# Straight code instead of loops on five engines, and a per-partition scalar in GpSimd's row normalisation, in an attention block with a LoRA mixture behind it

## The reference, cut to what matters

```python
x = x + attn(_layernorm(x), Wq, Wk, Wv, Wo, q_norm_w, k_norm_w)     # x: (2, 1024, 512)
x = x + lora_mixture(_layernorm(x), A, B, Wr, br)
...
q = rmsnorm(x @ Wq.T)      # 32 heads of 128
k = rmsnorm(x @ Wk.T)      # 8 heads of 128, each shared by 4 query heads
v = x @ Wv.T
scores = einsum(q, k) / sqrt(128) + alibi_bias          # causal
attn = softmax(scores)
out = einsum(attn, v) @ Wo.T
```

## Time and profile before

| | |
|---|---|
| timed runs | 2343.06, 2344.05, 2346.43 us; median 2344.05 us |
| span of the profiled execution | 2337.8 us |
| PE matmuls, busy | 2204.3 us, 94% of the span |
| PE weight loads, busy | 1901.5 us, 81% |
| DVE busy | 1403.3 us, 60% |
| ACT busy | 1185.4 us, 51% |
| POOL busy | 912.3 us, 39% |
| mean granted TensorE clock | 0.975 |
| DMA | 53.40 MB, 23 GB/s over the span |

### The profile page before, as it was taken

The page is one execution under the profiler, slowest core; times in us unless marked ns, Lnnn a source line. Parts: engine busy times, 40 slices in busy tenths (PEclk is TensorE's granted clock), DMA queues, the critical chain, the costliest instruction groups (busy, mean ns, idle before and its releaser), DMA issues.

```text
span 2337.8 us, 39513 instructions
## 1 busy us (share of the span) xinstructions
PE 2204.3 (94%) x12540; PEld 1901.5 (81%) x12540; DVE 1403.3 (60%) x3492; ACT 1185.4 (51%) x3397; POOL 912.3 (39%) x912
## 2 busy tenths in 40 slices
PE   6999999999999999999869999999999999999997
PEld 5887888878788887888668878787887888878885
DVE  4655656656565655656656556565565656656666
ACT  3554545555454555645235556454554545555552
POOL 3344343434343343444124434334343343434341
PEclk9999999999999999999989999999999999999999
DMA  3001010010101001010120010100001010010000
GB/s 118 19 1 46 1 46 1 13 34 1 46 1 43 4 1 46 1 46 1 47 67 7 1 46 1 47 1 28 19 1 46 1 46 1 1 46 1 1 1 37
DMA packets 27914, 53.40 MB, mean 23 GB/s; under 512 B 3033, under 2 KB 3033, under 8 KB 27745
## 3 DMA queue, kind: packets, MB, share of 16 engines
q1 hardware_dynamic: 26112, 50.34, 6.5%
q10 hardware_dynamic: 1632, 0.55, 0.1%
HBM read 46.68 MB, written 4.19 MB: 22 GB/s over the span
## 4 chain that ended last, share of the span: by engine, by line
PE 83%; issue 9%; POOL 4%; DVE 1%; ACT 1%; DMA 0%; ACTq 0%; POOLq 0%; DVEq 0%
PE s_ps L863 23%; PE turn_ps L855 17%; PE o_ps L863 16%; PE q_ps L863 14%; PE y_ps L863 13%; POOL probs L612 3%; DVE pT_lo L688 1%; ACT qn L531 1%; POOL q_inv_t L583 1%; DMA bias<-in_L_ffn_B 0%; ACT pT_hi L488 0%; POOL rstd L583 0%; POOL q_sum_eps_t L581 0%; PE q_ps L1013 0%; POOL bias L622 0%
## 5 line engine op out<-in xcount | busy, mean ns | idle before, releaser
L612 POOL TENSOR_TENSOR probs<-probs,p_inv_t 128x896 f32<-128x896 f32 (+7 forms) x512 | 576.7, 1147 | 724.7 <-DVE p_inv_t L756 724.7
L488 ACT ACTIVATE pT_hi<-turn_ps 128x512 fp32r<-128x512 f32 x576 | 332.7, 600 | 487.2 <-PE turn_ps L855 486.2
L748 DVE CUSTOM_DVE_ANT_0 probs<-s_ps,bias 128x896 f32<-128x896 f32 (+7 forms) x512 | 382.2, 753 | 187.2 <-issue 184.6
L688 DVE TENSOR_TENSOR pT_lo<-turn_ps,pT_hi 128x512 fp32r<-128x512 f32 x576 | 383.3, 686 | 142.9 <-ACT pT_hi L488 139.7
L525 ACT ACTIVATE probs<-probs,neg_max 128x896 f32<-128x896 f32 (+7 forms) x512 | 396.0, 774 | 81.0 <-DVE neg_max L748 80.8
L855 PE MATMUL turn_ps<-ident,probs 128*128 128x128 f32 x2560 | 364.7, 278 | 26.3 <-POOL probs L612 9.7
L855 PEld LDWEIGHTS turn_ps<-ident,probs 128*128 128x128 f32 x2560 | 309.6, 143 | 79.6 <-issue 16.6
L863 PE MATMUL s_ps<-kT_hi,qT_lo 128*128 128x512 f32 (+3 forms) x768 | 268.3, 349 | 50.0 <-issue 50.0
L863 PE MATMUL s_ps<-kT_hi,qT_hi 128*128 128x512 f32 (+3 forms) x768 | 280.2, 365 | 0.5 <-DVE qT_lo L690 0.5
L863 PE MATMUL s_ps<-kT_lo,qT_hi 128*128 128x512 f32 (+3 forms) x768 | 265.3, 345 | 0.0
L863 PE MATMUL o_ps<-pT_hi,v_hi 128*128 128x512 f32 x576 | 250.3, 434 | 12.2 <-DVE pT_lo L688 11.8
(11 more groups left out here) (98 smaller groups left out, 3976.6 us busy)
## 6 DMA issues: line engine op xcount, KB each, us to landing
wq_raw<-in_L_attn_Wq SPq DMA_DIRECT2D x16, 1024.0 KB, 6.7
wo_raw<-in_L_attn_Wo SPq DMA_DIRECT2D x16, 1024.0 KB, 5.4
y<-in_L_attn_x SPq DMA_DIRECT2D x16, 256.0 KB, 3.7
wkv_raw<-in_L_attn_Wk SPq DMA_DIRECT2D x16, 256.0 KB, 2.9
wkv_raw<-in_L_attn_Wv SPq DMA_DIRECT2D x16, 256.0 KB, 3.8
out<-y SPq DMA_DIRECT2D x16, 256.0 KB, 2.1
bias<-in_L_ffn_A ACTq DMA_DIRECT2D x1, 256.0 KB
bias<-in_L_ffn_B ACTq DMA_DIRECT2D x1, 256.0 KB
```

The source lines that it names most:

```text
L488: nc.scalar.activation(target, source, ACT.Copy).then_inc(sems["hi_done"], 1)
L612: nc.gpsimd.tensor_tensor(row, row, p_inv_t[:, s % 2, h:h + 1].to_broadcast((P, L)), ALU.mult).then_inc(sems["p_ready"], 1)
L688: nc.vector.tensor_tensor(target, source, high.bitcast(F32), ALU.subtract).then_inc(sems["lo_done"], 1)
L748: nc.vector.tensor_tensor_reduce(out=probs[:, s % 2, h, 0:L], in0=s_ps[:, at_col:at_col + L], in1=bias[:, h, S - L:S], scale=-1.0, scalar= ...
```

## The change

All hardware loops become Python loops, so each engine's program is written out in full, and every semaphore target is a constant. The lists of steps, the tiles and the waits stay as they are. Apart from that, POOL's `normalise` is another instruction: it had a second tensor, which is one column of `p_inv_t` read with a step of zero, and now has that column as a scalar for each partition.

```diff
@@ run_plans @@
-            with engine.Fori(0, NG - 1) as g:
+            for g in range(NG - 1):
                 run(GROUP, lambda name: group_at(name, b, g), lambda name: group_at(name, b, g),
                     *([g + 1] if with_group else []))
@@ sync @@
-                with sp.Fori(0, NG - 1) as g:
+                for g in range(NG - 1):
                     load_next(b, g, g + 1)
@@ scalar @@
-            with act.Fori(0, NB) as b:
+            for b in range(NB):
@@ gpsimd @@
-            with pool.Fori(0, NB) as b:
+            for b in range(NB):
                 layer_norm(lambda name: ln_at(name, b))
...
                         row = probs[:, s % 2, h, 0:L]
-                        nc.gpsimd.tensor_tensor(row, row, p_inv_t[:, s % 2, h:h + 1].to_broadcast((P, L)),
-                                                ALU.mult).then_inc(sems["p_ready"], 1)
+                        nc.gpsimd.tensor_scalar(row, row, p_inv_t[:, s % 2, h:h + 1], None, ALU.mult).then_inc(sems["p_ready"], 1)
@@ vector @@
-            with dve.Fori(0, NB) as b:
+            for b in range(NB):
@@ tensor @@
-            with pe.Fori(0, NB) as b:
+            for b in range(NB):
```

## The result

The changed kernel takes 2358.28 us (median of 4 runs, 2357.49 to 2360.53), the kernel before 2343.91 us (4 runs, 2343.06 to 2346.43). The ratio is 1.006, with a 95% interval of 1.0046 to 1.0074. The forecast was 2256 us and a range of 2243 to 2275, so it was wrong by 102 us and in its sign.

A forecast was written before the change was run, and what follows sets the result against it. The prediction took PE as the bound, its matmuls busy 2204.3 of 2337.8 us. Terms of 82.6, 1.6 and 3.6 made 87.8 us off the median of 2344.05, so 2256 us, with a range of 2243 to 2275.

The forecast's parts named there:

- POOL's new instruction: POOL's normalisation: priced like the affine select, 0.85 us less at 1024 columns; 3.6 us off in all, bounds 0 and 5.
- The sign of being wrong: In the changed kernel's profile: POOL's row over 2.3 us, with PE waiting for it at `turn.p.4.0` and `turn.p.6.0`.
- Rival (a): POOL's new instruction takes 1 + x times as long as the old; chance 0.06 up to x = 0.5, 0.04 beyond.
- some 1.5 for the rest: PE's added wait for slower POOL normalisations in tiles other than 4, 6 and 0, in us a group at x = 0.5.
- the point where it eats the whole gain: POOL's new instruction at x = 0.5, 1 + x times as long: 5.2 us a group, 83 us over 16 groups.
- The loops over groups: PE's branches back between groups: without them 6.88 us less a group, 12 times, 82.6 us; bounds 79.7 and 85.5.
- the group's first part: From a group's first transposes to its `y.0`: 14.62 us, taken from group 0 without its wait for normalised queries.
- The cause of the stall: PE at a group's start: any taken branch costs its instruction stream several us, at the branch and a few instructions behind the target.
- Rival (b): PE's stall is not the branch's and straight code has it too, as waits for instructions: near 2332 us; chance 0.04.
- The start of a group: Late `norm_q.1` or `max.0.0` once the stall is gone: charged nothing; if `norm_q.1` is late, some 3.6 us.
- rival (c): The stall goes, but half returns as waits for DVE or ACT at a group's start: 41 us, near 2297; chance 0.04.
- The end of batch 0: DVE's loop over batches branches and delays its statistics by 2.88 us; without it PE starts 1.6 us sooner, bounds 0 and 2.9.

The follow-up runs named there:

- the constant's: The changed kernel with POOL's normalisation multiplying by the constant 0.5 in place of the per-partition scalar: 2337.32 us, ratio 0.9978 to the kernel before.
- straight code with the old form: The changed kernel, all loops written out, but with the old two-input normalisation on POOL: 2247.83 us, ratio 0.9596 to the kernel before.
- the two kernels that split the engines: Old normalisation, against the kernel before: PE's program alone written out, 2249.43 us; all engines but PE written out, 2341.95 us.
- the one over two groups: All written out with the old normalisation, but PE keeps its batch loop and, after group 0, loops three times over two groups: 2254.91 us.
- tiles 2 and 3: All loops written out, the per-partition scalar in these tiles alone and the two-input form in the others: 2247.8 us, ratio 0.9593.
- one moved step: Written-out loops, two heads per old-form POOL instruction in tiles 0 to 6, plus `normalise.7.3` right behind `normalise.7.2` in the last group's plan: 2237.56 us.
- pairs alone: All loops written out, old two-input form, two heads in one POOL instruction in tiles 0 to 6: 2246.67 us, ratio 0.9588.

## Why the prediction was wrong, point by point

**The step that failed** is this one: "the nearest instruction with one tensor in and one out, the affine select, took 1038 ns for 1024. I take that". The term, POOL's new instruction, was to take 3.6 us off the time; the runs showed 110.5 us on top. The affine select isn't near to the tensor-scalar form in cost: 1038 against 2851 ns. The number of tensors read was the wrong likeness, and the constant's 2773 ns shows that the form's own pace is what counts. I had given only 0.10 to all cases in which the new form is slower, on that one row. The other row on POOL that I had was the two-input form itself, 1894 ns; the bounds of the term, 0 and 5 us, left out everything above it, and nothing in the trace excluded that. The sign of being wrong that the prediction named, over 2.3 us for a row and PE waiting at `turn.p.4.0` and `turn.p.6.0`, is what the profile shows.

**Rival (a) came about**, with x = 0.505, and its mechanism was right. It put the cost at 83 us for x = 0.5. From straight code with the old form to the changed kernel, PE's step to `turn.p.s.0` grew by 1.87 us in tile 4 (1.64 predicted), 1.72 in tile 6 (1.66), and 0.60 in tile 0 (0.38), each a mean over the groups. For the rest it allowed 1.5; tile 7's 1.43, tile 5's 0.54, tile 1's 0.44 and 0.42 ahead of the last query's transposes make 2.83. That is 7.0 a normal group, where a group measures 139.11 - 131.78 = 7.3 more; 14 of these are 103, and the two last groups add some 3.4 each. So the terms of the rival were mis-sized too, above all "some 1.5 for the rest", and "the point where it eats the whole gain" lies below x = 0.5: at 0.505 the new form took 110.8 us of a gain of 91.7.

**The loops over groups**: 82.6 us were forecast. A group is 131.78 in place of 139.15, so 7.37 and not 6.88, and 12 of them are 88.4. The mis-sized term is the group's first part, 14.62 from group 0, which is 14.08 between two groups. The bounds were 79.7 and 85.5, and the value lies outside of them. That it is PE's, as the prediction had it, is shown by the two kernels that split the engines.

**The cause of the stall** was put down to any branch taken, and this part of the reasoning is shown wrong. The branch back over the same body costs next to nothing when PE's program is moved by 40 instructions (2250.59 us, and 2249.43 with PE straight), and the one over two groups costs at most 1.8 us. What costs is the wait for instructions behind the jump when the body has to be fetched again, and its second part hangs on where the loop begins. The prediction cited the room for 2048 instructions and set it aside because of the sequencer's row; the row showed the price at this one position, not the rule. For the changed kernel the two readings gave the same time, so this error didn't move the forecast. Rival (b), the stall in straight code too, is refuted: the changed kernel has no such wait.

**The start of a group**, charged at nothing, held: no wait of PE for `norm_q.1` or `max.0.0` behind a group's end is seen in the straight kernel with the old form, so rival (c) is refuted.

**The end of batch 0**: 1.6 us were forecast. DVE's statistics stand right behind the last addition, as the timeline of the changed kernel shows:

```profile
1180.86 0.69 DVE L836 TENSOR_TENSOR y<-q_ps,y 128x512 f32<-128x512 f32 x1 [1.89 <-PE q_ps L1012]
1181.47 2.46 DVE L661 BATCH_NORM_STATS2 stats<-y 128x6 f32<-128x512 f32 x4
```

PE's wait for what comes of them, before and then after:

```profile
PE turn_ps L855 <- DVE probs L673: 9.4, 1, 9.4
```

```profile
PE turn_ps L854 <- DVE probs L672: 6.7, 1, 6.7
```

It fell by 2.7 us. With PE alone straight it is still 9.4, so this is DVE's branch. The eighth tile's transfer came sooner than assumed: in the straight kernel with the old form SP issues it at 1129.6, 2.1 us after the last addition ends (1127.53), where it was 1174.0 - 1171.04 = 3.0 before. The measured 2.7 is within the bound of 2.9, though not the 1.6 of the sum.

**The sum by what was measured**: in spans, 91.7 us off (2337.8 to 2246.1), of which 88.4 are the groups', 2.7 the batch's end and 0.6 not placed; and 110.8 on (2246.1 to 2356.9), so 19 us more. The medians say 14. The reason is the profiled execution of the kernel before: the time taken to lie around its span was 6.2 us, but every other run here has 1.8 or 1.9 between span and time, so that execution was some 4 us quicker than the median. The reason for the wrong sign is settled. What stays open is the exact rule by which PE's loop stays in or is fetched again: one position that keeps it (40) and two that don't (0 and 256) were run, and the place where it turns wasn't looked for.

## What to carry to other kernels

An instruction that the trace doesn't show has no price, and the nearest row may be near in the wrong property: measure the new form by itself before it goes where another engine waits within a few tenths of a us, or put it first where there is slack, as in tiles 2 and 3, where it cost nothing. An engine's busy share says nothing on this; list for each consumer how long after its producer it starts. If a hardware loop's branch costs several us on PE, look at how many instruction packets the profile counts: when they grow with the rounds, a few instructions more or less ahead of the loop may give what unrolling gives, as 40 did here. And look at what holds one short step back in a hand-written order: one moved step gave 9.1 us.

## What the runs showed of the hardware that was not expected

- On POOL the tensor-scalar multiply of f32 is slower than the tensor-tensor one with a broadcast operand: 2851 against 1894 ns for 128x1024, 608 against 400 for 128x128. With a constant it is 2773 and 531. The Trainium skill's page GPSIMD Engine Reference (Engine selection) calls one-input work on POOL roughly line-rate and two-input work some two times slower than VectorE's. The affine select, 1038 ns for 1024 columns, is in keeping with the first; for this multiply the rows show the reverse, and they decide.
- The kernel with the loops took 2343.91 us as it was, 2340.49 with 256 idle instructions ahead of PE's loop, and 2250.59 with 40. The branch of the loop over groups on PE's sequencer is 79 to 83 ns when not taken, 215 at the median when the target is in, and 3548 to 3764 at the median when it is fetched. A loop over PE's batches kept its fetch in the kernel moved by 40: 3927 ns.
- ACT's branch of the same loop takes 45 ns at the median, and the loops of the four engines other than PE cost nothing in the whole (ratio 1.0006).
- With pairs alone, PE's stop of 4.5 us in batch 0's last group leaves a granted clock of 0.83 over 20 us; in the changed kernel 42 stops of up to 1.7 us in batch 0 leave it at 1.00.
